# Selective scan on one core: states kept down the partitions, summed by swapped products and carried by one product per head

## The reference, cut to what matters

```python
xz = silu(in_proj_w @ x + in_proj_b);  x_ssm, res, gate = split(xz)
xf = silu(conv3(x_ssm) + dw_b)
dt, B_t, C_t = split(dbc_w @ xf + dbc_b)      # per head: 1 + 8 + 8 rows; dt = softplus(dt)
# each head (2) walks the 1024 tokens in an order of its own (perm)
h = exp(dt*A)[s] * h + dt*B_t[s] * x_t        # 128 channels x 8 states, per token
y_t = sum_s C_t[s] * h[s] + D * x_t
y = unpermute(y) * silu(gate) + res
out = x + silu(out_proj_w @ y + out_proj_b)
```

## Time and profile before

| | |
|---|---|
| median of 3 runs | 877.38 us (875.68 to 877.74) |
| the profiled execution: own time, span | 875.38 us, 872.9 us |
| granted clock of TensorE, mean | 0.96 of 2.4 GHz |
| PE busy | 794.8 us, 91% |
| DVE busy | 571.8 us, 66% |
| ACT busy | 557.0 us, 64% |
| POOL busy | 372.9 us, 43% |
| a phase in the middle (1 to 5) | about 97 us |
| start until the first chunk sums, last phase | 121 us, about 83 us |

### The profile page before, as it was taken

The page is one execution under the profiler, slowest core; times in us unless marked ns, Lnnn a source line. Parts: engine busy times, 40 slices in busy tenths (PEclk is TensorE's granted clock), DMA queues, the critical chain, the costliest instruction groups (busy, mean ns, idle before and its releaser), DMA issues.

```text
span 872.9 us, 11238 instructions
## 1 busy us (share of the span) xinstructions
PE 794.8 (91%) x3854; PEld 513.4 (59%) x3854; DVE 571.8 (66%) x1048; ACT 557.0 (64%) x1056; POOL 372.9 (43%) x325
## 2 busy tenths in 40 slices
PE   2689867999999999999999999999999999988996
PEld 1356557745675566645684576645684576654852
DVE  5798398467783769276774769275964759178724
ACT  6776645587647856587647846677648846654552
POOL 2394306760288107840388108840487008610240
PEclk9689858999999999999999999999999999999999
DMA  8824671567738293658638393749539463775242
GB/s 330 334 97 149 170 100 62 156 199 84 232 133 238 51 184 141 187 168 98 219 132 241 59 220 114 192 140 134 191 124 256 59 139 125 203 150 134 71 123 97
DMA packets 110986, 136.06 MB, mean 156 GB/s; under 512 B 41801, under 2 KB 91602, under 8 KB 110930
## 3 DMA queue, kind: packets, MB, share of 16 engines
q1 hardware_dynamic: 97040, 99.11, 44.8%
q0 software_dynamic: 12288, 35.80, 12.3%
q10 hardware_dynamic: 1602, 0.45, 0.3%
HBM read 82.76 MB, written 53.61 MB: 156 GB/s over the span
## 4 chain that ended last, share of the span: by engine, by line
PE 68%; ACT 11%; DVE 10%; issue 4%; POOL 4%; DMA 1%; SPq 0%; DVEq 0%; POOLq 0%
PE pj L1366 30%; PE pj L1491 9%; PE pj L1432 6%; PE st L1411 5%; PE tp L1386 5%; ACT big L630 4%; PE tp L1388 4%; PE pj L1442 3%; POOL xt_scratch L434 2%; ACT xf L610 2%; PE tp L1481 2%; DVE big L1121 2%; POOL crow L448 2%; PE tp L1422 2%; ACT L630 1%
## 5 line engine op out<-in xcount | busy, mean ns | idle before, releaser
L1366 PE MATMUL pj<-xb,inw 128*128 128x512 f32 x768 | 340.9, 598 | 0.0
L434 POOL DMA_INDIRECT xt_scratch<-stage,idx x128 | 175.6, 1372 | 344.3 <-issue 333.3
L1366 PEld LDWEIGHTS pj<-xb,inw 128*128 128x128 f32 x768 | 143.7, 191 | 167.0 <-issue 159.6
L448 POOL DMA_INDIRECT crow<-yt_scratch,idx x128 | 135.4, 1058 | 98.9 <-DMA yt_scratch<-rs 59.1
L1017 DVE SCALAR_TENSOR_TENSOR xf<-xs,small,xf 128x1024 f32<-128x1024 f32 x64 | 84.0, 1322 | 108.3 <-ACT xf L603 107.1
L1491 PE MATMUL pj<-gt,outw 128*128 128x512 f32 x256 | 118.2, 593 | 0.6 <-DVE gt L1171 0.6
L653 ACT COPY ch<-tp 128x256 f32<-128x256 f32 x128 | 42.7, 381 | 74.7 <-PE tp L1423 74.6
L1432 PE MATMUL pj<-xp,mblk 128*128 128x128 f32 x512 | 71.7, 285 | 17.0 <-ACT gt L685 8.8
L1177 DVE SCALAR_TENSOR_TENSOR xb<-xb,pcur,rs 128x1024 f32<-128x1024 f32 x32 | 41.0, 1284 | 60.3 <-ACT rs L716 60.3
L642 ACT COPY stage<-tp 128x256 f32<-128x256 f32 x128 | 47.8, 374 | 48.7 <-PE tp L1388 46.4
L1432 PEld LDWEIGHTS pj<-xp,mblk 128*128 128x128 f32 x512 | 64.7, 198 | 23.1 <-ACT gt L685 13.8
(11 more groups left out here) (241 smaller groups left out, 1151.6 us busy)
## 6 DMA issues: line engine op xcount, KB each, us to landing
xb<-in_x SPq DMA_DIRECT2D x16, 1024.0 KB, 7.1
xp<-xt_scratch SPq DMA_DIRECT2D x8, 2048.0 KB, 12.6
crow<-cd_scratch SPq DMA_DIRECT2D x128, 128.0 KB, 8.3
yt_scratch<-rs SPq DMA_DIRECT2D x16, 1024.0 KB, 4.9
out<-xb SPq DMA_DIRECT2D x16, 1024.0 KB, 5.6
gt<-in_x SPq DMA_DIRECT2D x4, 1024.0 KB, 11.7
big<-in_x SPq DMA_DIRECT2D x4, 1024.0 KB, 12.1
xp<-xt_scratch SPq DMA_DIRECT2D x8, 272.0 KB, 8.7
```

Of the source, the lines that this page charges most:

```text
L434: pool.indirect_dma_start(out=xt_d.ap(), out_offset=bass.IndirectOffsetOnAxis(ap=idx[:, k:k + 1], axis=0), in_=v(stage, (nt * H + h) * ROW ...
L448: pool.indirect_dma_start(out=v(crow, k * NB * P, (1, NB * P)), out_offset=None, in_=yt_d.ap()[0:(h + 1) * N], in_offset=bass.IndirectOffs ...
L1366: last = nc.tensor.matmul(o[:, :], v(inw, ct * 3 * C + col + ot * P, (1, P)), x_view(par, b, ct, nt * HALF, HALF), start=(ct == 0), stop=( ...
```

## The change

States are kept with image, block and state down the partitions (2 images x 8 blocks of 128 consecutive tokens x 8 states = 128) and the 128 channels along them, so that nothing needs to be turned but C.

* SyncE loads `xp` by place: a tile g now holds the g-th chunk of each of the 8 blocks. The dt of the natural order comes once more, with C, in a tile of its own, `cn`. There are 5 loads where there were 2, and 2 loads of `crow` where there were 16.
* `chunk_sums` swaps its operands: `bblk` (64 columns) is stationary and `xp` (128 columns) moving; the two images write the two halves of the partitions of `st`. A call does 4 places of both images (8 products), so there are still 4 calls of 8 products a phase.
* `scan` is one step per place on DVE: a copy and 7 `scalar_tensor_tensor` of 128 columns per head, each of which waits for the one before.
* `carry`: one product on PE with the matrix `cm` gives the state at the start of each block; `carried` (DVE, a copy and 7 `scalar_tensor_tensor` of 128 columns) adds it to the 8 states.
* `turn_c`: one transpose of C per head; `turned_factors` spreads the transposed C from the bank to `cblk`. The 16 transposes a head and ACT's copies L653 are gone.
* `segments` has 4 products (256, 32, 16 and 16 columns) for 3 (256, 128, 16); ACT has 2 small exponentials more per head; DVE's `softplus` works on 64 columns for 32.
* The order in `cycle` moves, on PE and DVE above all; in the first phase the routing's last chain goes behind the first head.
* In the start, ACT takes the statistics of 8 images in place of 10.

```diff
+            def chunk_sums(i, h, half):
+                ih = i * H + h
+                if half:
+                    pe.wait_ge(scan_step, ih * NT + 4)
+                else:
+                    wait(pe, states_ready, ih * NT)
+                    pe.wait_ge(x_rows_in[h], 16 * (i + 1))
+                    pe.wait_ge(bblk_ready, ih + 1)
+                for g in range(half * 4, half * 4 + 4):
+                    for b in range(NB):
+                        last = nc.tensor.matmul(v(st, g % 4 * P, (1, P), parts=CPT * S, p0=b * CPT * S),
+                                                v(bblk, (b * NT + g) * CPT * S, (1, CPT * S)), x_rows(h, b, g), start=True, stop=True,
+                                                skip_group_check=True)
...
+            def carry(i, h):
+                pe.wait_ge(carry_ready, ih + 1)
+                pe.wait_ge(scan_step, ih * NT + NT)
+                nc.tensor.matmul(v(st, 0, (1, P)), cm[:, :], v(hs[h], NT * P, (1, P)), start=True, stop=True).then_inc(carry_full, 1)
...
+            def scan(i, h, half):
+                for k in range(4):
+                    if g == 0:
+                        nc.vector.tensor_copy(state(h, 1), told).then_inc(scan_step, 1)
+                    else:
+                        dve.wait_ge(scan_step, ih * NT + g)
+                        nc.vector.scalar_tensor_tensor(state(h, g + 1), state(h, g), v(dcy, h * D_W + D_CHUNK + g, (1, 1)), told,
+                                                       ALU.mult, ALU.add).then_inc(scan_step, 1)
...
+            def carried(i, h):
+                dve.wait_ge(carry_full, ih + 1)
+                nc.vector.tensor_copy(state(h, 0), v(st, 0, (1, P))).then_inc(states_ready, 1)
+                for g in range(1, NT):
+                    nc.vector.scalar_tensor_tensor(state(h, g), v(st, 0, (1, P)), v(dcy, h * D_W + D_UPTO + g - 1, (1, 1)), state(h, g),
+                                                   ALU.mult, ALU.add).then_inc(states_ready, 1)
...
             def turned_factors(i, h):
+                dve.wait_ge(c_full, ih + 1)
+                wait(dve, r_full, ih * 2)
+                nc.vector.tensor_tensor(v(cblk, 0, (P, NT), (L, CPT), (1, L)), v(sg, CTURN, (1, NT), (0, CPT), (NT, L)),
+                                        const("own", (0, NT), (1, CPT), (0, L)), ALU.mult).then_inc(cblk_ready, 1)
```

More of the change, by code:

```diff
@@ L79, in constants @@
         diag=(r % L) == c[:, :L],
+        block=(r // L) == to_within, behind=(r // L) > to_within, earlier=(r // L) < c[:, :CPT], again=(0 * r + c[:, :H * Q]) % NT > 0, own=within == c[:, :CPT],
+        carry=(image == to_image) & (state == to_state) & (within < to_within),
         gridcol=np.concatenate([gx.reshape(NT, P).T, gy.reshape(NT, P).T], 1))
@@ L1221, in cycle @@
                 if more:
-                    begin(i + 1)
-                for b in range(NB):
-                    output(i, i % XB, b)
+                    factors(i + 1, 0)
+                output(i, i % XB, 0)
+                if more:
+                    turned_factors(i + 1, 0)
+                output(i, i % XB, 1)
             scores()
@@ L1271, in _ @@
             convolve(1, 1, (1,))
[L1272 to L1275 removed]
+            factors(0, 0)
             for i in range(PH):
@@ new lines, in within @@
+            def within(i, h, half, before):
+                for b in range(NB):
+                    o = pj_slot(2 * half + b, None, None, before)
+                    if half == 0 and b == 0:
+                        pe.wait_ge(mblk_ready, i * H + h + 1)
+                    for g in range(half * 4, half * 4 + 4):
+                        nc.tensor.matmul(v(o, g % 4 * P, (1, P)), v(mblk, (b * NT + g) * P, (1, P)), x_rows(h, b, g),
+                                         start=(g % 4 == 0), stop=False, skip_group_check=True)
@@ new lines, in from_states @@
+            def from_states(i, h, half):
+                ih = i * H + h
+                if half == 0:
+                    pe.wait_ge(cblk_ready, ih + 1)
+                pe.wait_ge(states_ready, ih * NT + half * 4 + 4)
+                for g in range(half * 4, half * 4 + 4):
+                    for b in range(NB):
+                        rows_of = dict(parts=CPT * S, p0=b * CPT * S)
+                        last = nc.tensor.matmul(v(pj[2 * half + b], g % 4 * P, (1, P)), v(cblk, g * P, (1, P), **rows_of),
+                                                v(hs[h], g * P, (1, P), **rows_of), start=False, stop=True, skip_group_check=True)
+                last.then_inc(r_full, 1)
@@ L1515, in cycle @@
                     rows(i + 1, 1, None, range(4, NT))
-                    before_t = (x_drained, (i + 2) * X_U)
-                for k in range(AHEAD):
-                    turn(i, 0, k, before_t)
-                before_t = (t_drained, i * T_U + AHEAD)
                 if i:
-                    gate(i, par, range(0, 4), last)
-                else:
+                    last = four(o_drained, i * O_U)
+                    gate(i, par, range(0, 2), last)
+                    carry(i, 0)
+                    gate(i, par, range(2, 4), last)
@@ new lines, in cycle @@
+                last = four(g_drained, i * G_U + 4)
+                if not i:
+                    last[3] = (chain_a, A_CHAIN + A_SIGMOID)
+                within(i, 0, 0, last)
+                if not i:
+                    carry(i, 0)
+                within(i, 0, 1, last)
+                turn_c(i, 1)
+                for half in range(2):
+                    from_states(i, 0, half)
+                last = four(r_drained, i * R_U + 4)
+                chunk_sums(i, 1, 0)
+                gate(i, par, range(4, 6), last)
```

472 lines of the change are left out of this document (229 added, 243 removed).

## The result

The changed kernel takes **919.2 us** in the median of 4 runs (918.5 to 921.0), the kernel before 876.5 us in the same series (875.3 to 877.7, 4 runs). The ratio is 1.049, 95% interval 1.047 to 1.051: **slower by 4.9%**. The forecast was 917 us, range 885 to 938. The profiled execution took 919.0 us, 917.2 of them span.

The account below looks back on a forecast made before the run. PE was taken to set the pace (busy 94.14 of 97.10 us in a middle phase), DVE close behind. Terms 26 + 6 + 3 + 5 = 40 on 875.4 gave 915.4; the median lies 2.0 higher: 917 us, range 885 to 938.

Parts of the forecast that it names:

- start: Before the first phase: DVE takes one more tile of two images, 2.4 us, while PE and ACT wait; +2 us.
- phase 0: First phase: `mblk` some 6 us sooner, but the second head's work stands in one DVE queue; +3 us (-3 to 8).
- phases 1 to 5: Middle phases: PE waits for `mblk` and the second head's scan, and the clock falls; +5.2 us each, +26 together.
- phase 6: Phase without a projection behind it: POOL and the loads are the path, scatters and results come later; +6 us (5 to 13).
- phase 7: Last phase: `carried` and `cm` delay the second head, the last store and gather begin later; +3 us (0 to 6).
- First head: Middle phase: `carried` ahead of `mblk` in DVE's queue delays it from 17.8 to 22.25; PE waits 6.7 us.
- Second head: Middle phase: PE waits 3.2 us for DVE's scan steps until 37.8; results end at 48.8, or 50.3 if the clock falls.
- What PE gets back: PE, middle phase: transposes of 4.0 us go, 0.7 is added, chunk sums save 2.6 us.
- B: Rival: same waits, but the clock hardly falls and chunk sums overlap better; 898 us (885 to 905), chance 0.22.
- C: Rival: POOL's scatters slow down beside many small pieces and `turn_back` waits; 935 to 950 us, chance 0.08.
- D: Rival: faster if PE gets the second head's scan bank before t = 33.4; 860 us (down to 835), chance 0.15.
- E: Rival: no change in time, because gain and wait cancel; chance 0.05.

Follow-up runs that it names:

- clock_kept_short: Changed kernel with 7 unused PE products ahead of the first head's `within` in phases 1 to 6, filling the wait: 909.2 us, ratio 1.040 to the kernel before.
- carry_first: Changed kernel with PE doing the first head's carry ahead of gates 0 to 3 in phases 1 to 7: 902.0 us, ratio 1.032 to the kernel before.
- bias_weights_carried: Changed kernel with DVE doing all bias additions, then the first head's token weights and `mblk`, then `carried`: 890.2 us, ratio 1.018 to the kernel before.
- scan_ahead: bias_weights_carried with the second head's first scan call moved ahead of turned factors and token weights on DVE: 865.0 us, ratio 0.989 to the kernel before.
- after: The changed kernel itself, without further edits: 919.2 us, ratio 1.049 to the kernel before.
- cblk_last: scan_ahead with the second head's turned factors behind its last scan steps (phases 1 to 7) and phase 0's carry ahead of `within`: 856.1 us, ratio 0.978.
- clock_kept: Changed kernel with 14 unused PE products ahead of the first head's `within` in phases 1 to 6: 947.1 us, ratio 1.083 to the kernel before.
- sums_by_half: Changed kernel with each chunk-sums call issuing 8 instructions for one image, then 8 for the other, instead of alternating: 915.8 us, one execution.

## Why the prediction was right

**The size is right, and mostly for the stated reasons.** The terms of the sum, forecast and measured:

| term | forecast | measured |
|---|---|---|
| start | +2 | -1.7 |
| phase 0 | +3 | +7.2 |
| phases 1 to 5 | +26 (5 x 5.2) | +26.3 |
| phase 6 | +6 | +7.7 |
| phase 7 | +3 | +4.9 |
| span | +40 | +44.4 |

**First head.** Gates at t = 8.3 (measured 8.4), carry in DVE's hands at 12.15 (12.3), eight operations 0.27 apart (0.26), token weights at 14.75 (14.7), `mblk` at 22.25 (22.2), wait 6.7 (6.76), low clock about 1.5 (`within` 5.58 against 3.81 in clock_kept_short, 1.8). carry_first and bias_weights_carried show that this wait is caused by the place of `carried` in DVE's queue: each moves it by the amount by which DVE is moved.

**Second head.** DVE waits for `from_states` (1.81), the scan steps release PE at 37.8 (38.0), wait 3.2 (3.25), results at 48.8 or 50.3 (48.4 where the clock held). I had left open whether this wait lowers the clock and priced a fall at 1.5. The rows say: in phases 2 and 4 it did not, in 3 and 5 it did, and those are 4.0 longer (104.4 against 100.4): the chunk sums and two gates behind the wait take 7.6 instead of 4.6, and `within` of the first head, at the other wait, 6.5 instead of 5.6. Phase 1 lies between. Two errors of opposite sign met in the 5.2: the phase without a second fall is +3.4 where I had +4.4, the one with it +7.4 where I had +6.0. The mean is right partly by luck.

**What PE gets back.** 6.2 us a phase, forecast 5.9, and it does reach the time once the order is mended: 97.0 - 92.8 = 4.2 a phase. A call of chunk sums took 1.02 (1.09 forecast). The Trainium skill (TensorEngine Tiling, "Performance Considerations") puts this swap at 2x column tiling; here it is 1.73 / 1.02 = 1.7, and 1.14 if the halves don't alternate.

**Phases 6 and 7** are 1.7 and 1.9 above the forecast, inside the ranges given. Phase 6 is the path that was named: SyncE's queue issues the loads 50.8 us into the phase instead of 43.8, and DVE gets dt 10.5 us after the first of them instead of 9:

```profile
790.81 3.77 SPq L362 DMA_DIRECT2D cn<-xt_scratch  x1
794.62 2.92 SPq L370 DMA_DIRECT2D xp<-xt_scratch  x2
```

```profile
801.31 0.28 DVE L1061 SCALAR_TENSOR_TENSOR dts<-xp 128x16 f32<-128x16 f32 x2 [14.40 <-DMA xp<-xt_scratch]
```

7.0 of the 7.7 are there before the loads are issued: POOL's scatters start 5.5 later in the phase than before (15.8 for 10.3) and end 7.5 later (44.8 for 37.3). scan_ahead, with the same loads, has 83.1. For phase 7 I named `carried` and `cm` in DVE's queue and the gates that stand ahead of the results. The row there is a wait of 3.27 for DVE's scan steps at 862.30, and scan_ahead, which leaves the gates where they are, has 82.5: the gates don't cost the +4.9. But the queue alone doesn't either. Of the 5.2 between after and scan_ahead only 1.2 are waiting (PE idle for 17.8 and 16.6); 4.0 are PE time at a lower clock (busy 69.9 at 0.90, and 65.9 at 0.96), which I had not priced in this phase.

**Start and phase 0** are where the steps failed, though their sum is near (+5.5 against +5). At the start the additional statistics on DVE didn't show: the first chunk sums stand 1.7 earlier, and over all kernels with this start they lie at 119.1 to 121.2, so nothing of a loss of 2 shows, and a gain of 1.7 isn't established (the two kernels with the old start have 121.1 and 122.0). In phase 0 I had `mblk` some 6 us sooner with the wait gone. It came 3.9 sooner (18.9 into the phase, not 22.8), but the wait is 6.51 and not 0, because PE is there 5.5 sooner as well (12.4 instead of 17.9): the turns are gone, and the 2.7 us of bias products that it used to do ahead of it now stand behind the second head's scan. That head waits 7.56 for scan steps, which stand in DVE's queue behind `carried`, the routing chain and the token weights:

```profile
138.25 3.59 PE L1496 MATMUL pj<-xp,mblk 128*128 128x128 f32 x16 [6.51 <-DVE mblk L1198]
...
162.02 1.97 PE L1471 MATMUL st<-xp,bblk 128*64 128x128 f32 x16 [7.56 <-DVE hs L1109]
```

I had listed that queue and not added it up. scan_ahead shortens the phase by 3.6; the rest against the 102.1 of before is 3.7 (2.4 in cblk_last). There is still a wait of over 8 us for the first `mblk` in it, which I did not take apart.

**The rivals.** B (clock hardly falls, 898) is refuted by the 0.92 in the windows and by clock_kept_short. C (POOL behind) did not happen: the last gather of phase 4 is issued at 605.85; PE's `turn_back` products at 613.0 don't wait, and the next ones, at 614.5, wait 0.44 for DVE. D (faster) had its decision point at the second head's scan before t = 33.4. In scan_ahead PE has its bank at t = 27.5 (537.41 in the phase from 509.88), and the kernel is faster: the place was the right one, and it took another order of DVE's queue to get there. E (no change) is excluded by the interval.

## What to carry to other kernels

An engine with a third of its time free can still set the time, and then the order of its queue is worth more than the work that a change saves: the same instructions gave 919 and 856 us. When a change makes a queue wait for something new (here DVE for a product on PE), list what stands behind the wait and who needs it first, and put what is needed soonest and doesn't depend on it ahead. Price a wait of PE with what it does to the clock behind it: here about two thirds of the loss in a middle phase came from instructions at the low clock.

## What the runs showed of the hardware

**DVE and POOL kept each other out.** In each of phases 1 to 5 of clock_kept the second head's `mblk` met POOL's four scalings of the images. DVE's row and POOL's in phase 5:

```profile
700.36 7.27 DVE L1198 TENSOR_TENSOR mblk<-m,cst 128x2048 f32<-128x2048 f32 x1
```

```profile
700.77 4.71 POOL L441 TENSOR_SCALAR xb<-xb,pcur 128x1024 f32<-128x1024 f32 x4
```

The same product takes 2.29 in after (its row starts at 573.11, POOL's scaling there at 580.06). 7.27 (7.27 to 7.29 in the five phases) is about 2.29 + 4.71: by its length, one waits for all of the other. The Trainium skill (SBUF — State Buffer, "SBUF: two separate sides") states this for a DVE operation with two SBUF inputs against a GpSimd operation that reads SBUF, a lock held for the whole instruction by whichever starts first. The trace agrees on the size. On who goes first its rows stand differently: DVE's row starts 0.41 to 0.44 ahead of POOL's first, and yet four of POOL's instructions in a row went through before DVE finished. So a delay on one engine can make two others meet, and cost one of them five more microseconds; PE waited for 0.9 to 2.6 of it in four of the five phases.

**The granted clock behind a short wait is not decided by the length of the wait alone.** The second head's wait was 3.25 to 3.30 in after, carry_first and clock_kept_short. It was followed by chunk sums at half the full clock (1.2 of 2.4 GHz) in phases 3 and 5 of after, phase 4 of carry_first and phases 1 to 4 of clock_kept_short, where PE had been busy instead of idle 14 us earlier. In phase 3 of carry_first neither of two waits of 3.3 was followed by a fall. Behind 2.77 in sums_by_half the clock was at the full level in phases 1 to 5. But a shorter wait is no safe one: behind the 1.85 of cblk_last it held in phases 1, 2, 3 and 5 and fell in phase 4 (93.7 us with PE busy for 89.6, against 92.0 and 87.9 in phase 5), and behind the 3.05 of scan_ahead it fell in three of five. What decides between them these runs don't show. So the length of a single phase can mislead about an edit by several microseconds.
